# T1 by accumulating DMA in 18 more steps of a two-layer autoencoder kernel on one core

## The reference

```python
def _L0_rec_ref(x, W_enc, b_enc, W_dec, b_dec):
    B, L, D, F = (1024, 2, 1024, 4096)
    f = jax.nn.relu(jnp.einsum('bld,ldf->bf', x, W_enc) + b_enc)
    x_hat = jnp.einsum('bf,lfd->bld', f, W_dec) + b_dec
    return x_hat
```

## Time and profile before

| | us |
|---|---|
| median of 3 runs | 662.78 |
| lowest and highest | 662.36, 664.5 |
| profiled execution, its own time | 662.21 |
| span of its trace | 660.4 |
| PE busy | 644.8 (98%) |
| DVE busy | 571.8 (87%) |
| ACT busy | 336.9 (51%) |

### The profile page before, as it was taken

How to read it: one execution, slowest core, us unless ns; L and a number is a source line. 1 busy time by engine, 2 the same in 40 slices (tenths; PEclk the granted TensorE clock), 3 DMA queues, 4 the chain that set the end, 5 groups by cost and what they waited for, 6 DMA issues and landing times.

```text
span 660.4 us, 8015 instructions
## 1 busy us (share of the span) xinstructions
PE 644.8 (98%) x2892; PEld 524.7 (79%) x2892; DVE 571.8 (87%) x749; ACT 336.9 (51%) x423; POOL 17.4 (3%) x25
## 2 busy tenths in 40 slices
PE   7899999999999999999999999999999999999996
PEld 4677888888887888888888888788877888888885
DVE  6999989879999856659897599999999999998854
ACT  4455335354565445455665657545555445464452
POOL 0100000000000000000000000001100011011000
PEclk8999999999999999999999999999999999999999
DMA  8985564654465464545545465569955589589624
GB/s 329 386 241 192 194 216 168 226 195 150 159 208 183 168 224 159 190 151 185 182 149 196 141 232 189 186 214 252 275 183 192 192 233 267 208 211 314 205 100 181
DMA packets 43958, 135.81 MB, mean 206 GB/s; under 512 B 5136, under 2 KB 5136, under 8 KB 43920
## 3 DMA queue, kind: packets, MB, share of 16 engines
q1 hardware_dynamic: 41184, 126.40, 54.7%
q0 software_dynamic: 2736, 8.91, 7.3%
HBM read 122.18 MB, written 4.19 MB: 191 GB/s over the span
## 4 chain that ended last, share of the span: by engine, by line
PE 82%; DVE 14%; issue 2%; ACT 1%; DMA 0%; SPq 0%; DVEq 0%; ACTq 0%
PE sums L602 26%; PE sums L604 26%; PE sums L603 26%; DVE w_split L390 6%; PE sums L615 3%; DVE w_raw L390 3%; DVE forms L390 2%; DVE s_sum L390 2%; DVE place L390 1%; DMA w_raw<-w_enc 0%; ACT w_split L287 0%; ACT place L327 0%; ACT place L340 0%; DVE place L557 0%; ACT forms L358 0%
## 5 line engine op out<-in xcount | busy, mean ns | idle before, releaser
L287 ACT CAST w_split<-w_raw 128x1024 fp32r<-128x1024 f32 (+1 forms) x255 | 239.7, 945 | 289.0 <-PE sums L604 198.4
L602 PE MATMUL sums<-w_split,forms 128*128 128x512 f32 x896 | 354.9, 396 | 9.2 <-DVE w_split L390 7.5
L604 PE MATMUL sums<-w_split,forms 128*128 128x512 f32 x896 | 349.9, 391 | 0.0
L603 PE MATMUL sums<-w_split,forms 128*128 128x512 f32 x896 | 349.5, 390 | 0.0
L390 DVE TENSOR_TENSOR w_split<-w_raw,w_split 128x1024 fp32r<-128x1024 f32 (+1 forms) x257 | 269.0, 1083 | 60.6 <-ACT w_split L287 59.8
L602 PEld LDWEIGHTS sums<-w_split,forms 128*128 128x128 f32 x896 | 168.6, 188 | 52.1 <-issue 13.8
L604 PEld LDWEIGHTS sums<-w_split,forms 128*128 128x128 f32 x896 | 168.5, 188 | 35.9
L603 PEld LDWEIGHTS sums<-w_split,forms 128*128 128x128 f32 x896 | 168.8, 188 | 33.6
L390 DVE TENSOR_TENSOR w_raw<-w_raw 128x512 f32<-128x512 f32 x252 | 173.4, 688 | 6.8 <-DMA w_raw<-w_dec 2.5
L390 DVE TENSOR_TENSOR place<-place,sums 128x1024 f32<-128x1024 f32 x25 | 29.3, 1215 | 6.3 <-PE sums L604 4.3
L390 DVE TENSOR_TENSOR forms<-s_sum,forms 128x512 fp32r<-128x512 f32 x48 | 32.9, 685 | 0.2
(11 more groups left out here) (23 smaller groups left out, 65.7 us busy)
## 6 DMA issues: line engine op xcount, KB each, us to landing
w_raw<-w_dec SPq DMA_DIRECT2D x96, 512.0 KB, 4.2
w_raw<-w_enc SPq DMA_DIRECT2D x94, 512.0 KB, 4.2
w_raw<-w_enc SPq DMA_DIRECT2D x36, 256.0 KB, 2.8
w_raw<-w_dec SPq DMA_DIRECT2D x32, 256.0 KB, 2.8
place<-place POOLq DMA_DIRECT2D x15, 512.0 KB, 8.0
place<-xT SPq DMA_DIRECT2D x8, 512.0 KB, 8.8
outT<-place SPq DMA_DIRECT2D x16, 256.0 KB, 2.1
w_raw<-w_raw POOLq DMA_DIRECT2D x4, 256.0 KB, 6.5
```

The costliest lines, as they stand in the source:

```text
L287: nc.scalar.copy(split(s, q, 0), w_pos(s, 2 * q, n)).then_inc(hi_done, 1)
L602: nc.tensor.matmul(out, v_hi, w_hi, start=k == 0 and n != UNBROKEN + 1, stop=False)
L603: nc.tensor.matmul(out, v_lo, w_hi, start=False, stop=False)
L604: last = nc.tensor.matmul(out, v_hi, w_lo, start=False, stop=k == PAIRS - 1 and n != UNBROKEN)
```

## The change

T1 becomes an accumulating DMA in the 18 steps of four products in which forms are made or which lie between such steps, 26 to 31 and 90 to 101, beside steps 4 to 7. POOL issues T1(26) to T1(31) and T1(90) to T1(92) before the folds of chunk 10, and T1(93) to T1(101) after them. DVE leaves one sum out in each of the 18 steps, and DVE and ACT wait for the landing of T1(s) in place of it.

```diff
+
+    EARLY_T1 = [range(4, PAIRS), range(26, 32), range(90, 93)]
+    LATE_T1 = [range(93, 102)]
+
     def by_dma(s):
-        return 4 <= s < PAIRS
+        return any(s in steps for steps in EARLY_T1 + LATE_T1)
+
+    def t1_count(s):
+        return 16 * sum(by_dma(t) for t in range(s % RAW, s + 1, RAW))
...
-            for s in range(PAIRS):
-                if by_dma(s):
-                    pool.wait_ge(w_loaded[s % RAW], 32 * (s // RAW + 1))
-                    pool.dma_start(w_pos(s, 1), w_pos(s, 0),
-                                   accum_op=ALU.add).then_inc(w_summed[s % RAW], 16)
+            def t1(s):
+                pool.wait_ge(w_loaded[s % RAW], 32 * (s // RAW + 1))
+                pool.dma_start(w_pos(s, 1), w_pos(s, 0),
+                               accum_op=ALU.add).then_inc(w_summed[s % RAW], 16)
+
+            for steps in EARLY_T1:
+                for s in steps:
+                    t1(s)
...
                 fold(y12, U3)
                 fold(y22, U3)
+                if kind == "dec2":
+                    for steps in LATE_T1:
+                        for s in steps:
+                            t1(s)
...
                 if by_dma(s):
-                    act.wait_ge(w_summed[s % RAW], 16)
+                    act.wait_ge(w_summed[s % RAW], t1_count(s))
...
                 if by_dma(s):
-                    dve.wait_ge(w_summed[s % RAW], 16)
+                    dve.wait_ge(w_summed[s % RAW], t1_count(s))
```

## The result

| | before | after |
|---|---|---|
| median, us | 662.64 (4 runs, 662.36 to 664.5) | 675.6 (4 runs, 675.24 to 676.06) |
| profiled execution, us | 662.21 | 675.38 |
| span of its trace, us | 660.4 | 673.6 |

The ratio is 1.0199, with a 95% interval of 1.0187 to 1.021: the changed kernel is slower by 13 us. The forecast was 679.0, with a range of 674.3 to 683.5, in which the measured time lies.

The account below looks back on a forecast made before the run. PE, busy 98% of the span, was taken as the bound, with DVE holding it in steps 95 to 101. 662.2 + 15.8 + 2.4 - 1.6 = 678.8, 679.4 as median, rounded to 679.0 us; range 674.3 to 683.5.

Parts of the forecast that it names:

- The stall: PE waits 15.8 us ahead of step 92, since T1(93) is issued on POOL only behind all five folds.
- three times 3.75: Folds 1 to 3, queued behind T1(92), each add 3.75 us, so fold 3 lands at 472.0.
- fold 5's time: Fold 5 lands 9.7 us after fold 4's issue, at 482.0, with T1(93) 2.2 us behind it.
- The clock: After the stall TensorE's clock comes back at its lower level, costing 2.4 us, between 1.7 and 3.4.
- The gain of 1.60: In steps 95 to 101, where DVE holds PE up, less DVE work saves 1.60 us if every T1 lands in time.
- Steps 26 to 31: PE never waits for DVE there, so six sums fewer gain 0 and the DMAs cost 0.
- The break after step 33: 1.21 us lost on PE, paced by ACT's copy and casts; unchanged, gain 0, at most 1.21.
- The slot's loop: Load, issue, T1, two sums and two lo take 16.25 us per three steps, against PE's 16.32; it just holds.
- T1(93) isn't held behind folds 4 and 5: Rival, chance 0.12: T1(93) isn't held behind fold 5 in q0 and lands at 480.5; 675.3 us, or 674.6.
- Interference: Rival, chance 0.13: transfers slow each other, adding 3.4 us to the stall and 1.5 to the loop; 683 to 684 us.
- The early clearing of the folds: Rival, chance 0.04: folds land early, T1(93) lands by 468.4 or 469.2, no stall; 661.2 or 662 us.

Follow-up runs that it names:

- kept_busy: Changed kernel with 54 matmuls of zeros on PE ahead of step 92, filling the stall; 674.81 us, ratio 1.0186 to the kernel before.
- t93_first: Changed kernel with T1(93) also issued ahead of the folds, T1(94) to T1(101) behind them; 674.61 us in a single execution.
- t93_mid: Changed kernel with T1(93) issued between the landing of fold 3 and the issue of fold 4; 670.67 us in a single execution.
- folds_last: Changed kernel with T1(93) to T1(101) also issued ahead of the folds, so all 18 T1s stay DMAs; 662.58 us, ratio 0.9999 to the kernel before.
- three: Changed kernel cut to T1 by DMA in steps 4 to 7 and 90 to 92; 661.71 us, ratio 0.9989 to the kernel before.
- five: Changed kernel cut to T1 by DMA in steps 4 to 7, 90 to 92, and 98 and 99 behind the folds; 661.48 us, ratio 0.9987 to the kernel before.
- to_98: Changed kernel cut to T1 by DMA in steps 4 to 7 and 90 to 98, all ahead of the folds; 662.26 us, ratio 0.9997 to the kernel before.
- first_six: Changed kernel cut to T1 by DMA in steps 4 to 7 and 26 to 31; 662.25 us, ratio 0.9995 to the kernel before.
- nine: Changed kernel cut to T1 by DMA in steps 4 to 7, 90 to 92 ahead of the folds, 96 to 101 behind; 664.61 us, ratio 1.0031 to the kernel before.

## Why the prediction was right, point by point

**The stall.** Forecast 15.8 us, measured 13.0: PE starts step 92 at 484.31 for 471.19, of which 0.1 was there before step 92. Step by step, forecast and measured: T1(92) issued 454.2 and 454.58; fold 3 landed 472.0 and 456.20 + 16.17 = 472.4; T1(93) issued 474.0 and 473.73; T1(93) landed 484.2 and 481.5. Until its issue the chain was right to 0.4 us, in part by luck: from the landing of T1(92) at 461.0 the three folds added 2.5, 3.8 and 5.1 us, where the sum had three times 3.75. The term that was too large is the last: T1(93) landed 2.7 us earlier than in my sum, though issued only 0.3 earlier. I had taken fold 5's time from the earlier trace rows, where two loads ran beside it, and allowed for their absence only in T1(93). With DVE held, no load was issued from 466.7 to 485.3, and fold 5 landed 6.9 us after its issue for 9.2 before:

```profile
place<-place POOLq DMA_DIRECT2D x1, 512.0 KB, 6.9
w_raw<-w_raw POOLq DMA_DIRECT2D x1, 256.0 KB, 7.8
```

The other traces say the same: fold 5 took 6.9 to 7.4 us in the three kernels that held DVE with all folds ahead (this one, kept_busy, t93_first), 9.1 to 12.3 in the nine that didn't hold DVE so long, the kernel before among them, and 7.8 in t93_mid, behind T1(93). A stall also removes the traffic that I had priced its transfers with.

**The clock.** Forecast 2.4 us between 1.7 and 3.4; step 92 lost 1.64, and kept_busy shows a net 1.0. Its sign and place were right, the size was under my lower end.

**The gain of 1.60.** In the changed kernel steps 95 to 101 ran at 38.10 us, a gain of 1.58. The forecast made it hang on a condition, "Gain 1.60, if every T1 lands in time", and gave no reason why they would; that it was met here is partly luck. Without a stall, in one trace each, those steps gained 1.28 us in folds_last (given back behind them), 0.53 in three and 0.04 in five, and lost 0.58 in to_98, because DVE waited for T1s. The slow step 92 isn't what brought the gain (kept_busy). Whether the stall was, in which T1(94) and T1(95) landed while DVE stood still, is likely but not shown.

**Steps 26 to 31.** Forecast 0, measured 0 (first_six, 0.9995). The break after step 33 stayed at 13.44 us, paced by ACT as forecast.

**The slot's loop** of 16.25 us for 16.32. PE had no gap in steps 26 to 31 here, so it held there; its length as such wasn't measured. The T1s of steps 26 to 31 and 96 to 101 took 3.7 to 8.2 us, 5.4 on average, for the 6.3 to 7.0 in the earlier trace rows. The long ones make single steps late, and a late step isn't won back where DVE has no lead.

**Sum.** 679.0 less 2.7 for fold 5 and T1(93) and 0.8 for the clock is 675.5; measured 675.6. That it closes this well is partly chance: the forecast put 0.6 us between the profiled execution and the median, where this kernel has 0.2, and the rounding down from 679.4 took the 0.4 back.

**The rivals.** That T1(93) isn't held behind folds 4 and 5 is excluded by t93_mid, and by the landings of 482.9 and 484.2 of T1(94) and T1(95), 1.4 us apart behind T1(93). Interference was real, with little effect on this time and a large one on whether the gain comes. The early clearing of the folds didn't happen; by the page's figures (the Trainium skill, DMA: Bandwidth & Descriptors, "Anatomy of one DMA — SWDGE (gpsimd) path") it would have, and fold 3 would have landed 3.2 us after its issue as an estimate, for 16.2 us queued here.

## What to carry to other kernels

A wait in an in-order queue is a wait for everything behind it: before moving work to a lightly used engine (POOL was 3% busy), write down what stands in its queue with the times, and compare with when the moved work is wanted. An addition of 0.69 us that becomes a DMA of 4 to 8 us pays only if its consumer would otherwise be late and yet starts that long after the load; where the consumer is the bound it mostly waits for the DMA instead. Of all kernels here three and five came out lowest, 0.1% below the kernel before, with intervals that end at 0.9997 and 0.9996; all 18 T1s in the best order tried only came back to its time.

## What the runs showed of the hardware

**A T1 that is issued together with a load lands later.** I tabulated the 126 T1s from step 8 on that overlap no fold, over all traces, by how long before them the first half of the latest load was issued (a load up to 0.3 us behind them counts as together). Less than 1.0 us: 45 T1s, mean 7.1 us to landing, 5.7 to 8.2. Between: 22, mean 6.2, 4.7 to 8.4. More than 1.6 us: 59 T1s, mean 4.8, 3.3 to 7.7. Two of them in the changed kernel, T1(26) at 139.73 with load(27) 0.25 us behind it, and T1(28) at 151.86 with load(28) 6.4 us before:

```profile
139.98 0.33 SPq L209 DMA_DIRECT2D w_raw<-w_enc  x1
...
w_raw<-w_raw POOLq DMA_DIRECT2D x1, 256.0 KB, 8.2
...
w_raw<-w_raw POOLq DMA_DIRECT2D x1, 256.0 KB, 3.9
```

That it is the sharing of the DMA engines is likely but wasn't tried by itself.

**TensorE's clock** fell to its lower level at 473.9 in the changed kernel, by the trace's record of the granted clock, PE's last matmul before the stall having ended at 471.5 (471.08 + 0.39). It stood there until 487.6, and PE had started again at 484.31 (the matmuls of 0.63 us in the timeline of PE above end there). The times differ from kernel to kernel: in t93_mid PE stopped at the same 471.4 and the clock fell only at 476.8, and in nine, where PE was idle from 488.0 to 491.4, it fell at 492.2, with PE at work again. Matmuls of zeros onto an open sum kept it at 1.00 throughout, from 466 to 492.
